# Attention scores from two scaled fp16 parts in 50 rows: one score product instead of two, the ScalarE copies of one maximum in eight left out

## The reference

```python
mod = (silu(c) @ wmod).reshape(2, 6, 1, 256)            # shift, scale and gate, for attention and for the MLP
h = layernorm(x) * (1 + ca) + sa
Q, K, V = (lora_linear(h, W, b, A, B) for q, k, v)      # 16 heads of 16 channels
attn = softmax(Q @ K.T / 4)                             # 2 x 16 heads, each 2048 x 2048
x = x + ga * lora_linear(attn @ V, Wo, bo, Ao, Bo)
h = layernorm(x) * (1 + cb) + sb
x = x + gb * (shared_swiglu(h) + swiglu of the one expert that the gate chooses for the token)
```

## Time and profile before

| | |
|---|---|
| median of 3 runs | 1809.66 us (1807.82 to 1810.91) |
| profiled execution: its time, its span | 1808.66 us, 1806.4 us |
| PE busy | 1787.7 us, 99% of the span, 13143 matmuls |
| ACT busy | 1471.6 us, 81% |
| DVE busy | 1384.0 us, 77% |
| POOL busy | 366.8 us, 20% |
| projections | 0 to about 134 us |
| exponentials with the maxima pass beside them | about 134 to 1322 us |
| exponentials alone (the last head and a third) | about 1322 to 1366 us |
| output projection, MLP and experts | from about 1366 us |

### The profile page before, as it was taken

How to read it: one execution, slowest core, us unless ns; L and a number is a source line. 1 busy time by engine, 2 the same in 40 slices (tenths; PEclk the granted TensorE clock), 3 DMA queues, 4 the chain that set the end, 5 groups by cost and what they waited for, 6 DMA issues and landing times.

```text
span 1806.4 us, 35954 instructions
## 1 busy us (share of the span) xinstructions
PE 1787.7 (99%) x13143; PEld 808.0 (45%) x13144; DVE 1384.0 (77%) x2719; ACT 1471.6 (81%) x1908; POOL 366.8 (20%) x452
## 2 busy tenths in 40 slices
PE   9999999999999999999999999999999999999997
PEld 5533333333333333333333333333326555799996
DVE  7789999999999999999999999999935432355553
ACT  6559999999999999999999999999997411244442
POOL 6755020030000000000000200001010177233332
PEclk9999999999999999999999999999999999999999
DMA  7443131232121121111313111123114723322221
GB/s 239 133 137 99 36 91 47 83 101 62 61 70 35 44 59 58 53 35 47 93 52 91 54 44 45 44 76 90 35 65 174 289 96 119 126 72 65 67 69 41
DMA packets 91363, 148.83 MB, mean 82 GB/s; under 512 B 19749, under 2 KB 57830, under 8 KB 91085
## 3 DMA queue, kind: packets, MB, share of 16 engines
q1 hardware_dynamic: 82428, 122.83, 22.5%
q0 software_dynamic: 7792, 22.57, 3.8%
q10 hardware_dynamic: 992, 1.44, 0.2%
HBM read 95.88 MB, written 51.41 MB: 82 GB/s over the span
## 4 chain that ended last, share of the span: by engine, by line
PE 93%; DVE 3%; ACT 2%; issue 1%; POOL 1%; DMA 0%; POOLq 0%; DVEq 0%; ACTq 0%
PE ps L1301 27%; PE ps L1289 24%; PE ps L1232 15%; PE ps L2086 8%; PE ps L1622 6%; PE ps L2109 3%; PE ps L1959 3%; PE ps L767 2%; PE ps L1652 2%; PE ps L786 1%; ACT prob L1435 1%; DVE mx L1354 1%; PE ps L2065 0%; POOL rest L990 0%; PE ps L1261 0%
## 5 line engine op out<-in xcount | busy, mean ns | idle before, releaser
L1435 ACT ACTIVATE prob<-ps 128x1024 f32<-128x1024 f32 x1024 | 992.6, 1021 | 3.2 <-issue 1.5
L1354 DVE TENSOR_REDUCE mx<-ps 128x1 f32<-128x512 f32 x1343 | 876.0, 686 | 112.4 <-PE ps L1232 108.3
L1232 PE MATMUL ps<-k_high,q_high 64*128 64x512 bf16 x1803 | 576.5, 381 | 0.9 <-DVE mx L1354 0.2
L1301 PE MATMUL ps<-prob,vs 128*32 128x512 f32 x4096 | 545.5, 605 | 0.2 <-ACT head_out_sb L1441 0.2
L1289 PE MATMUL ps<-q_high,k_high 64*128 64x512 bf16 x2048 | 489.9, 376 | 0.5 <-ACT prob L1435 0.3
L1289 PE MATMUL ps<-q_low,k_low 34*128 34x512 bf16 x2048 | 490.2, 377 | 0.0
L1232 PEld LDWEIGHTS ps<-k_high,q_high 64*128 64x128 bf16 x1803 | 142.8, 94 | 342.4 <-DVE mx L1351 180.3
L1289 PEld LDWEIGHTS ps<-q_low,k_low 34*128 34x128 bf16 x2048 | 143.3, 94 | 118.6
L1464 POOL CAST mb<-turned_sb 16x128 bf16<-16x128 f32 x32 | 9.0, 281 | 817.2 <-ACT turned_sb L1421 805.3
L1351 DVE CUSTOM_DVE_ANT_0 step_sb<-ps,step_sb 128x512 f32<-128x512 f32 x245 | 169.1, 690 | 3.3 <-PE ps L1232 0.7
L1289 PEld LDWEIGHTS ps<-q_high,k_high 64*128 64x128 bf16 x2048 | 143.5, 95 | 54.3 <-ACT prob L1435 18.9
(11 more groups left out here) (187 smaller groups left out, 1771.5 us busy)
## 6 DMA issues: line engine op xcount, KB each, us to landing
k_high<-qk_parts SPq DMA_DIRECT2D x126, 128.0 KB, 2.8
qk_parts<-parts SPq DMA_DIRECT2D x32, 384.0 KB, 3.0
k_low<-qk_parts SPq DMA_DIRECT2D x128, 64.0 KB
q_high<-qk_parts SPq DMA_DIRECT2D x126, 64.0 KB, 2.7
head_out<-head_out_sb SPq DMA_DIRECT2D x31, 256.0 KB, 2.2
sorted_in<-zero_row POOLq DMA_DIRECT2D x13, 390.0 KB, 4.0
xs<-sorted_in SPq DMA_DIRECT2D x39, 130.0 KB
q_low<-qk_parts SPq DMA_DIRECT2D x128, 32.0 KB
```

Of the source, the lines that this page charges most:

```text
L1232: pe.matmul(ps[:, ring.bank((n, m, u)), :], q_high[p][mine, t * P:(t + 1) * P], keys, start=True, stop=True).then_inc(s_max, 1)
L1301: mm = pe.matmul(ps[32 * j:32 * j + 32, 7, :], vs[buf(h)][:, kt, :], prob[:, (kt + 1) % 2, j * CH:(j + 1) * CH], start=(kt == 0), stop=(kt ...
L1354: dve.tensor_reduce(largest, bank, AX.X, ALU.max).then_inc(s_ring, 1)
L1435: act.activation(prob[:, (kt + 1) % 2, :].rearrange("p (u c n) -> p u c n", u=2, c=2)[:, :, half, :], ps[:, bank:bank + 2, :], ACT.Exp).th ...
```

## The change

A query or key is now multiplied with a power of two that is computed on the chip, and split into two fp16 parts; a score is a single product of 50 rows: first times first, second times first, first times second part, and the two rows of the maximum, whose key rows hold 2^15. The maxima pass uses 48 of these rows. The exponential multiplies by `restore`, one value per partition, which takes the powers of two back. `k_low` and `q_low` go, with their DMA loads. So do `carried`, `unit_sb` and L1414: those banks are reduced by VectorE directly. The differences of keys (`k_step`) are kept, and the order in `turn` is not touched. In the projections `middle` and the third part go, and a chain over all engines computes the powers of two before the first `take` (`largest_w`, `square_sums`, `bound`, `root_bound`, `unit_scale`).

```diff
-                    self.add((n, m, u), "act" if steps_of(n, m, u) or carried(n, m, u) else "dve", count)
+                    self.add((n, m, u), "act" if steps_of(n, m, u) else "dve", count)
...
-            dve.tensor_scalar(bqk[:, 0:2], bqk_in[:, 0:2], 0.25, None, ALU.mult)
-            dve.tensor_copy(bqk[:, 2:4], bqk_in[:, 2:4])
...
-            moments(dve, step, 1)
+            dve.wait_ge(s_weff, 2)
+            dve.tensor_reduce(largest_w[:], wqkv[:, 0:2], AX.X, ALU.max, apply_absolute_value=True).then_inc(s_range, 1)
+            gather(dve, step, 1, 0, TPC)
+            dve.wait_ge(s_range, 3)
+            dve.tensor_reduce(bound[:], ps[:, 7, 0:4 * HALF].rearrange("p (m f) -> p m f", m=2), AX.X,
+                              ALU.add).then_inc(s_range, 1)
+            moments(dve, step, 1, gathered=TPC)
+            dve.wait_ge(s_range, 5)
+            step(dve.tensor_scalar(unit_scale[:].bitcast(U32), root_bound[:].bitcast(U32), EXPONENT, EXPONENT,
+                                   ALU.bitwise_and, ALU.bitwise_xor))
...
-        def middle(act, n):
-            act.wait_ge(s_rest, n + 1)
-            act.copy(parts[n % SLOTS][:, 1, :], rest[n % UQ][:]).then_inc(s_mid, 1)
...
-                bank, scale = 2 + n % 2, 0.25 if o < 2 else 1.0
+                bank, scale = 2 + n % 2, unit_scale[:, o // 2:o // 2 + 1]
...
+            act.wait_ge(s_range, 4)
+            act.activation(root_bound[:], bound[:], ACT.Sqrt, bias=eps[:, 0:1],
+                           scale=2.0 / PART_UNIT ** 2).then_inc(s_range, 1)
             root(act, 1)
+            act.wait_ge(s_range, 6)
...
-            for part in range(2):
-                at = slice(u * HROWS + part * LROWS, u * HROWS + (part + 1) * LROWS)
...
+            wide = slice(u * HROWS, u * HROWS + LROWS)
+            last = slice(u * HROWS + LROWS, u * HROWS + PROWS)
+            eng.dma_start(q_high[p][wide, :], q_parts[0:2, mine, cols].rearrange("a d t -> d a t")).then_inc(done, 16)
+            eng.dma_start(k_high[p][wide, :], k_parts[0:1].to_broadcast([2, B * D, S])[:, mine, :]
+                          .rearrange("a d t -> d a t")).then_inc(done, 16)
+            eng.dma_start(q_high[p][last, :], q_parts[0, mine, cols]).then_inc(done, 16)
+            eng.dma_start(k_high[p][last, :], k_parts[1, mine, :]).then_inc(done, 16)
...
-            for low, (keys, queries) in enumerate(((k_high[p], q_high[p]), (k_low[p], q_low[p]))):
-                for u in (1 - i, i):
-                    mine = slice(u * HROWS, u * HROWS + (LROWS + 2 if low else HROWS))
-                    mm = pe.matmul(ps[:, bank + u, :], keys[mine, kt * P:(kt + 1) * P],
-                                   queries[mine, i * CH:(i + 1) * CH], start=(low == 0), stop=(low == 1))
+            for u in (1 - i, i):
+                mine = slice(u * HROWS, u * HROWS + SROWS)
+                mm = pe.matmul(ps[:, bank + u, :], k_high[p][mine, kt * P:(kt + 1) * P],
+                               q_high[p][mine, i * CH:(i + 1) * CH], start=True, stop=True)
...
-            if carried(*what):
-                act.wait_ge(s_max, ring.made(what))
-                wait(act, s_carried, earlier(carried, who, first + 1))
-                act.copy(unit_sb[:], bank).then_inc(s_turned, 1)
...
-                                   ps[:, bank:bank + 2, :], ACT.Exp).then_inc(s_exp_free, 1)
+                                   ps[:, bank:bank + 2, :], ACT.Exp, scale=restore[:, 0:1]).then_inc(s_exp_free, 1)
```

More of the change, by code:

```diff
@@ L57 @@
 HROWS = 4 * DH
+PROWS = 3 * DH
+SROWS = PROWS + 2
+MAX_UNIT = 2.0 ** 15
+PART_UNIT = 2.0 ** 11
+EXPONENT = 0x7F800000
 LROWS = 2 * DH
@@ L283, in block_kernel @@
         qf = buffers("qf", [P, CH], F32, r, UQ)
-        parts = buffers("parts", [P, 3, CH], BF16, r, SLOTS)
+        parts = buffers("parts", [P, 2, CH], F16, r, SLOTS)
+        r.at = max(r.at, top - E * 4 * FC * D + CPB * 4 * TPC * D)
+        largest_w = r("largest_w", [P, 2, HALF])
+        col_squares = r("col_squares", [P, 2, HALF, B])
+        row_squares = r("row_squares", [P, 2, 2 * HALF])
+        bound = r("bound", [P, 2])
+        root_bound = r("root_bound", [P, 2])
+        power = r("power", [P, 2])
+        unit_scale = r("unit_scale", [P, 2])
         stats = buffers("stats", [P, TPC, 6], F32, r)
@@ L528, in moments @@
         def moments(dve, step, g, gathered=0):
-            gather(dve, step, g, gathered, TPC)
+            if gathered < TPC:
+                gather(dve, step, g, gathered, TPC)
             hold(dve)
@@ L791, in project_tensor @@
             qk(0, 0)
+            pe.wait_ge(s_range, 2)
+            pe.matmul(ps[:, 7, 0:4 * HALF], ones[:], row_squares[:].rearrange("p m f -> p (m f)"), start=True,
+                      stop=True).then_inc(s_range, 1)
             pe.wait_ge(s_weff, 2)
@@ L1099, in stack @@
             load_key_steps(eng, h)
-            for u in range(2):
-                stack_low(eng, h, u)
         def maxima(sp, h):
@@ L1344, in reduce_pair @@
                 what = (n, m, u)
-                if steps_of(*what) or carried(*what):
+                if steps_of(*what):
                     continue
@@ L1404, in carry @@
             bank = ps[:, ring.bank(what), :]
-            if steps_of(*what):
-                k = earlier(steps_of, who, first + 1)
-                act.wait_ge(s_max, ring.made(what))
-                if k:
-                    act.wait_ge(s_ring, step_folded[k - 1])
-                act.activation(step_sb[:], bank, ACT.Relu).then_inc(s_turned, 1)
-            if carried(*what):
-                act.wait_ge(s_max, ring.made(what))
-                wait(act, s_carried, earlier(carried, who, first + 1))
-                act.copy(unit_sb[:], bank).then_inc(s_turned, 1)
+            if not steps_of(*what):
+                return
+            k = earlier(steps_of, who, first + 1)
+            act.wait_ge(s_max, ring.made(what))
+            if k:
+                act.wait_ge(s_ring, step_folded[k - 1])
+            act.activation(step_sb[:], bank, ACT.Relu).then_inc(s_turned, 1)
         def take_turned(act, n):
@@ L1420, in take_turned @@
             wait(act, s_mb, n)
-            act.copy(turned_sb[:], ps[0:KT, ring.bank(what), 0:P]).then_inc(s_turned, 1)
+            act.activation(turned_sb[:], ps[0:KT, ring.bank(what), 0:P], ACT.Copy, scale=1.0 / MAX_UNIT
+                           ).then_inc(s_turned, 1)
         def attend_scalar(act):
             act.sem_inc(s_hstore, 16)
+            act.wait_ge(s_range, 7)
             def exps(n, kt):
@@ L1501, in following @@
                     zero(n + 1 - NB * (E + 1) + E)
-            fill_ones(pool, step, 2)
             for n in range(1, NB):
```

156 lines of the change are left out of this document (61 added, 95 removed).

## The result

The changed kernel takes 1823.05 us (median of 4 runs, 1821.70 to 1824.19), the kernel before 1808.84 us in the same comparison: ratio 1.0077, 95% interval 1.0062 to 1.0092. It is slower by 14 us; 1780 was forecast, and the range ended at 1805.

What follows compares the result with a forecast made beforehand. TensorE was taken to lead at 4.81 us a couple; afterwards the handover loop, 4.59, with extras 4.72. 1808.66 - 31.6 (attention) + 3.7 (last tiles) - 1 (projections) = 1779.8, about 1780 us; own range 1766 to 1793, 8-in-10 range 1748 to 1805.

Steps and rivals of the forecast that it cites:

- the second half of the loop: On TensorE, single maxima product to next pair: 1.09 us, taken as 1.30 less one slot of 0.215.
- the loop: In attention, handovers between TensorE, VectorE and ScalarE over three banks: 2.42 + 2.17 = 4.59 us a couple (two iterations).
- the third reduction: In a copy iteration, VectorE's third reduction since the pair frees the bank for the next pair, at 2.42 us.
- TensorE leads before with 2.40 us an iteration: In attention of the kernel before, TensorE leads at 4.81 us a couple; ScalarE has 4.65 of work, VectorE 4.27.
- ScalarE's operand: Scale from memory adds 0.085 us to each exponential's distance; as a rival costing 0.18, about 1850 us, chance 0.05.
- ScalarE's 4.51 us a couple: ScalarE's work in attention after the change: 4.17 + 4 x 0.085 us; as the leader, 1753 us, ScalarE-leads chance 0.24.
- The once-a-head extras: Per head in attention: output copy +0.42, transposition +0.51, 0.1 kept from before; 1.03 / 8 = 0.13 us a couple.
- The last 22 tiles: From 1322 to 1366 us, without reductions, ScalarE leads: 44 exponentials at +0.085 each, +3.7 us.
- The projections: At the start, powers of two delay the first take to about 15.5 us (+1.5), relief elsewhere; net -1 us.
- The slower side: Whole kernel slower than before, chance 0.13: longer handovers 0.06, ScalarE's operand 0.05, slots 0.02.
- longer handovers: Rival in the attention loop: late products pay extra weight loads, 4.90 to 5.08 us a couple; 1824 us, chance 0.06.
- the slots of fp16: Rival on TensorE: 50-row fp16 products cost more than a slot, couple 4.94 us, about 1834 us, chance 0.02.

Runs made afterwards that it cites:

- the second experiment: Kernel before with the 34-row score products, third parts and maximum left out and a constant exponential scale: 1792.76 us, ratio 0.9918.
- the last experiment: Changed kernel with the single maxima product ahead of the weighting and its reduction left out from the third head on: 1743.37 us, ratio 0.9660.
- the constant: Changed kernel with the exponential's scale a constant (2^-40) and not read from memory: 1816.32 us, ratio 1.0047.
- the register: Changed kernel with the exponential's scale read once into a register of ScalarE: 1812.37 us, ratio 1.0045.
- the third experiment: Changed kernel with the single maxima product (half 1) and the transposition issued behind the weighting, not ahead of it: 1956.57 us, ratio 1.0830.

## Why the prediction was wrong

**The step that failed** is the second half of the loop: "the next pair is 1.30 - 0.215 = 1.09 behind it (808.13 to 809.43, less the slot for which that product stood behind a low score in its rows)". There was no such slot. From the single product to the next pair it is 1.31 us in the changed kernel, in both kinds of iteration and in the kernel with the copies back, whether or not a score product went out with it, and swapping the rows changed nothing. I had read 1.74 us for six products and the weighting as four slots and 0.86; it is two slots to the single product (0.44), 0.31 from there to the weighting, and 1.00 from the weighting to the pair, and the last two are one piece: in the trace TensorE starts nothing else in them. The error stands in the loop twice a couple; 0.22 us of it reaches the step iteration in full, and 0.05 the copy iteration, where I had the third reduction at 2.42 us as the bound.

**What the loop is with the right number.** Copy iteration: 0.42 + 0.69 + 0.05 = 1.16 to the single product, 1.31 behind it, 2.47 (measured 2.486). That is longer than the 2.42 which I had for the third reduction, so the loop changes its path: not the ring as a whole, but the one bank that VectorE gives back, and then the weighting that stands behind the product in TensorE's order. Step iteration: 0.43 + 0.60 + 0.05 + 1.31 = 2.39 (measured 2.390). Together 4.86 against 4.59 forecast and 4.81 before. The mechanism, the product ahead of the weighting that waits for its own iteration's first bank, was the forecast's; its price decided the sign.

**Step by step.**
- *TensorE leads before with 2.40 us an iteration:* the time was right, its composition not. Without the two slots of the low products 2.41 - 0.44 = 1.97 us of its own are left (I had 3.95 a couple), and it does not lead. Nor did it lead by much before: the loop of handovers stood right behind it, 0.42 + 0.60 + 0.05 + 1.31 = 2.38 us with ScalarE's copy or positive part as the releaser, and the second experiment measured 2.378 and 2.390. The prediction took the loop up for the changed kernel alone.
- *ScalarE's operand:* 0.085 us a distance forecast. The duration went from 1023 to 1113 ns; the bounds were 83 and 97 ns. In the last heads, where exponentials are back to back, the distance is (6.14 - 1.11) / 5 = 1.006 against (3.91 - 1.02) / 3 = 0.96 before, where some waited, and 0.92 where none did:

```profile
1344.76 6.14 ACT L1419 ACTIVATE prob<-ps,restore 128x1024 f32<-128x1024 f32 x6
```

```profile
1331.71 3.91 ACT L1435 ACTIVATE prob<-ps 128x1024 f32<-128x1024 f32 x4 [0.33 <-PE ps L1289]
```

  Right in size. It is worth 5 to 6 us in this kernel and 49 with the copies (1840.06 to 1790.58). ScalarE's 4.51 us a couple was right too: the last experiment, where it leads, has 4.50.
- *The once-a-head extras:* I put 0.93 us on the output copy and the transposition and kept 0.1, 1.03 a head. The iteration with the transposition is 2.62 us for 2.39, and the step iteration after the output copy 2.506 for 2.390: 0.35 us. 0.68 us a head, 21 us in all, was too much, and hid part of the first error: with 4.86 and my extras I would have said 1846.
- *The last 22 tiles:* +3.7 us forecast, as ScalarE was busy for 42.2 of 44 us. Measured 2.036 us a tile before, 2.047 after: +0.3. TensorE set them before (the row of before above has a wait of 0.33 us for the scores), ScalarE sets them now (six exponentials without a gap in the row of after), and without the 34-row products and with a short exponential they fall to 1.89. There too I took a busy share for a lead.
- *The projections:* the first take was forecast at 15.5 us and stands at 15.26, 1.3 later than before:

```profile
11.77 1.22 DVE L673 TENSOR_REDUCE largest_w<-wqkv 128x4 f32<-128x1024 f32 x1
...
13.67 0.30 PEld L806 LDWEIGHTS ps<-row_squares,ones 128*128 128x128 f32 x2 [1.01 <-POOL row_squares L996]
...
15.26 0.78 ACT L875 ACTIVATE qf<-ps,bqk,unit_scale 128x512 f32<-128x512 f32 x1
```

  The reduction of 1024 columns took 1.22 us as forecast. By the first weighting the 1.3 us are made up again (-0.12 us, for -1 forecast, where kernels with the same projections differ by 1 us). That ScalarE's and GpSimd's relief does it is likely; no run separates it.
- *The slower side* was in the prediction with 0.13, by other mechanisms: longer handovers (1824 us, right in size by accident; the handovers were as read, 0.42 for 0.46), ScalarE's operand (refuted by the constant and the register, which leave the kernel slower than before), the slots of fp16 (0.22 us for 50 rows, as taken).

What stays open: why the weighting doesn't start until 0.31 us behind the single product. 0.22 of it is that product's own slot; the change of the array's shape (64 rows to 32 columns) may be the rest, but no run here has the weighting behind a product of its own shape. Nor does a run give the ring a fourth bank: that three banks are one too few for four products is argued from the third and the last experiment.

## What to carry to other kernels

When products are taken from the engine that seems full, follow the chain of handovers that is left, with the distances between starts, and check each distance on two places of the trace that differ in what you subtract from it: I had one place, and 0.2 us of it decided the sign. An in-order engine with a long instruction (the weighting, 1.3 us with what it needs around it) and a ring in which a product needs the bank that its own turn has just filled pays the whole handover in every turn, so the releaser of that one bank should be the fastest one with room; whether a copy helps or harms is decided by what ScalarE has beside it. A scale that is the same in all partitions is cheaper for ScalarE in a register than in memory.

## What the runs showed of the hardware

- A scale that ScalarE reads from memory adds 90 ns to an exponential of 1024 columns (1113 against 1023 ns, 0.086 us from start to start), one in a register nothing (1023). The Trainium skill ("ScalarE: Activation LUTs", What ACT_TABLE_LOAD costs) has 93 ns for the operand; the runs agree.
- In the trace products of 512 columns start in twos, within 10 ns of each other, and the next two 0.22 us later. The two need not be on different halves of the rows (804.14 and 804.15 in the third experiment are half 0 and the first score, both on rows 0 to 63), and swapping the order of the halves made a ratio of 1.0002.
- Two products of 34, 48, 50 or 64 rows, bf16 or fp16, take the same slot of 0.22 us.
- From the last product of 34 to 64 rows to the weighting in 32-column groups it is 0.31 us (0.306 to 0.316 as the median of each kernel run here), from there to the next product of 48 or 64 rows 1.00 us.
